# First attention: two transposed thirds of the weights ahead of the next scores, the projections behind the last third, the subtraction in two halves

## The reference, cut to what matters

```python
x = _layernorm(x + _L0_attn_ref(x, L0_attn_W_Q, L0_attn_W_K, L0_attn_W_V, L0_attn_W_O, L0_attn_b_Q, L0_attn_b_K, L0_attn_b_V, L0_attn_virtual_k, L0_attn_virtual_v), axis=-1)
x = _layernorm(x + _L0_xattn_ref(x, ctx_768, ...), axis=-1)
...
```

## Time and profile before

| | before |
|---|---|
| median of three runs | 4582.13 us |
| the profiled execution | 4580.66 us |
| its span in the profile | 4578.9 us |
| first scores (L275) to last | 152.5 to 867.5 us |
| TensorE busy, share of the span | 84% |
| mean granted TensorE clock | 0.92 |

### The profile page before, as it was taken

The page is one execution under the profiler, slowest core; times in us unless marked ns, Lnnn a source line. Parts: engine busy times, 40 slices in busy tenths (PEclk is TensorE's granted clock), DMA queues, the critical chain, the costliest instruction groups (busy, mean ns, idle before and its releaser), DMA issues. The chain is left out here.

```text
span 4578.9 us, 84527 instructions
## 1 busy us (share of the span) xinstructions
PE 3831.4 (84%) x33378; PEld 2565.5 (56%) x33378; DVE 2800.7 (61%) x7503; ACT 2112.3 (46%) x3569; POOL 1172.6 (26%) x819
## 2 busy tenths in 40 slices
PE   0688888888899879998999996654779999598999
PEld 0466666566556556664555554433547776465665
DVE  9577777666899756666565554985242222476555
ACT  4466666544333225555555544441364444354332
POOL 3444444222344311002455452321110000010000
PEclk9999999999999859999999998776689999798999
DMA  2222222100000001000000000003300000000000
GB/s 93 45 49 48 47 47 48 22 1 1 1 1 1 1 12 41 2 1 1 2 2 2 2 2 1 15 21 114 121 1 1 1 1 1 28 2 2 1 10 10
DMA packets 59436, 91.90 MB, mean 20 GB/s; under 512 B 16306, under 2 KB 42628, under 8 KB 57796
## 3 DMA queue, kind: packets, MB, share of 16 engines
q1 hardware_dynamic: 54916, 80.88, 7.5%
q10 hardware_dynamic: 4128, 5.64, 0.4%
HBM read 42.30 MB, written 10.62 MB: 12 GB/s over the span
## 5 line engine op out<-in xcount | busy, mean ns | idle before, releaser
L853 PE MATMUL banks<-XT,weight_region 128*128 128x512 f32 x1696 | 781.2, 599 | 2.3 <-DVE T L1229 2.3
L875 PEld LDWEIGHTS banks<-weight_region,HT 128*128 128x128 f32 x4672 | 560.5, 192 | 151.5 <-issue 91.7
L1252 DVE SCALAR_TENSOR_TENSOR x_res<-banks,WT,x_res 128x128 f32<-128x128 f32 x1056 | 297.1, 343 | 489.4 <-PE banks L875 449.6
L875 PE MATMUL banks<-weight_region,HT 128*128 128x128 f32 x4672 | 570.1, 276 | 21.6 <-DVE HT L1240 15.2
L853 PEld LDWEIGHTS banks<-XT,weight_region 128*128 128x128 f32 x1696 | 305.8, 193 | 288.5 <-issue 283.2
L1005 ACT ACTIVATE HT<-banks,weight_region 128x512 f32<-128x512 f32 x256 | 173.1, 687 | 240.0 <-PE banks L853 233.7
L1068 POOL TENSOR_TENSOR FNM<-FNM,FRS 128x8 f32<-128x8 f32 x16 | 4.6, 286 | 1014.4 <-ACT FRS L964 1014.4
L458 DVE TENSOR_REDUCE MX<-banks 128x8 f32<-128x1152 f32 x128 | 173.1, 1352 | 115.8 <-PE banks L275 113.8
L384 ACT COPY PT<-banks 128x384 f32<-128x384 f32 x384 | 171.4, 480 | 131.5 <-PE banks L285 129.7
L1643 ACT COPY PT<-banks 77x512 f32<-77x512 f32 x256 | 142.8, 582 | 186.9 <-PE banks L1565 186.8
L1096 POOL TENSOR_TENSOR T<-T,T 128x512 f32<-128x512 f32 x128 | 162.6, 1272 | 210.6 <-ACT T L1028 208.1
(11 more groups left out here) (472 smaller groups left out, 8589.7 us busy)
## 6 DMA issues: line engine op xcount, KB each, us to landing
FL<-RAW SPq DMA_DIRECT2D x512, 64.0 KB, 2.3
T<-s4d_k_dram SPq DMA_DIRECT2D x8, 1024.0 KB, 5.8
weight_region<-in_l_ffn__w_dram SPq DMA_DIRECT2D x2, 2048.0 KB, 8.6
film_dram<-F SPq DMA_DIRECT2D x8, 512.0 KB, 2.9
weight_region<-in_l_ffn__w_dram ACTq DMA_DIRECT2D x2, 2048.0 KB
FO<-film_dram SPq DMA_DIRECT2D x8, 512.0 KB, 4.1
x_res<-in_x_dram SPq DMA_DIRECT2D x1, 2048.0 KB
weight_region<-in_l_ffn__w_dram SPq DMA_DIRECT2D x2, 1024.0 KB, 10.6
```

The lines of the kernel that those rows point to most:

```text
L853: nc.tensor.matmul(PS[:, q % 4, :], w, xt, start=True, stop=True).then_inc(s.h_ps, 1)
L875: ins = nc.tensor.matmul(PS[:, 4 + u % 2, b * P:(b + 1) * P], HT[:, u % 2, j, b * P:(b + 1) * P], w2[j], start=j == 0, stop=j == len(w2) - 1)
L1252: ins = nc.vector.scalar_tensor_tensor(R[:, t, :], PS[:, 4 + u % 2, b * P:(b + 1) * P], WT[:, t, e:e + 1], R[:, t, :], ALU.mult, ALU.add)
```

## The change

TensorE, step n: T0 and T1 of step n-2 come first, then the scores of step n, then T2, then the due items, then both mixes. The ring's order is T0, T1, T2, items. ScalarE copies T0, T1 and T2 ahead of the items. VectorE subtracts in two halves, banks 0 and 1 (new semaphore `sub_a`), then banks 2 and 3 (`sub`); TensorE's project and first two mask matmuls wait for `sub_a`, the last two for `sub`.

```diff
-                order += [("T0", n - 2), ("T1", n - 2)]
+                order += [("T0", n - 2), ("T1", n - 2), ("T2", n - 2)]
             order += due(n)
-            if n >= 2:
-                order.append(("T2", n - 2))
...
                     if n >= 1:
-                        pe.wait_ge(s.sub, n)
+                        pe.wait_ge(s.sub_a, n)
                     if n >= 2 * NR and n % NR == 0:
                         project(n // NR - 2)
                     for i in range(4):
+                        if i == 2 and n >= 1:
+                            pe.wait_ge(s.sub, n)
                         nc.tensor.matmul(PS[:, i, 0:2 * K], IDB[:], MASK[:].rearrange("p a k -> p (a k)"), start=True, stop=False)
...
                 for n in range(N + NR + 1):
+                    live = 2 <= n < N + 2
+                    if live:
+                        weights_T(n - 2, 0)
+                        weights_T(n - 2, 1)
                     if n < N:
                         scores(n)
                     elif n % NR == 0:
                         pe.wait_ge(s.sub, N)
                         project(n // NR - 2)
-                    live = 2 <= n < N + 2
                     if live:
-                        weights_T(n - 2, 0)
-                        weights_T(n - 2, 1)
+                        weights_T(n - 2, 2)
                     for item, p in due(n):
                         produce(item, p)
                     if live:
-                        weights_T(n - 2, 2)
                         mix(n - 2, 0)
-                    if live:
                         mix(n - 2, 1)
...
                     if live:
                         weights(3 * (n - 2))
                         weights(3 * (n - 2) + 1)
+                        weights(3 * (n - 2) + 2)
                     for item, p in due(n):
                         take(item, p)
-                    if live:
-                        weights(3 * (n - 2) + 2)
...
-                    nc.vector.tensor_tensor(SM[:, n % 3, 1:9, :].rearrange("p (a i) k -> p i a k", a=2), sc[:, :, :, 0:P],
-                                            bc(MX[:, n % 2].unsqueeze(3), [P, 4, 2, P]), ALU.subtract).then_inc(s.sub, 1)
+                    main = SM[:, n % 3, 1:9, :].rearrange("p (a i) k -> p i a k", a=2)
+                    for h, done in ((0, s.sub_a), (2, s.sub)):
+                        nc.vector.tensor_tensor(main[:, h:h + 2], sc[:, h:h + 2, :, 0:P], bc(MX[:, n % 2, h:h + 2].unsqueeze(3), [P, 2, 2, P]),
+                                                ALU.subtract).then_inc(done, 1)
```

More of the change, by code:

```diff
@@ L185, in due @@
         return [(item, n // NPR + 1) for item in TAKE[n % NPR]] if n // NPR + 1 < NP else []
-    with sublayer(nc, "cst vkc one xt_ps xt kq_ps raw flip0 flip1 cosm sinm rot v_ps v s_ps mx sub ex pt_ps pt z_ps shuf lnz rz zt o_ps res" + LN) as (s, ctx):
+    with sublayer(nc, "cst vkc one xt_ps xt kq_ps raw flip0 flip1 cosm sinm rot v_ps v s_ps mx sub_a sub ex pt_ps pt z_ps shuf lnz rz zt o_ps res" + LN) as (s, ctx):
         sb = E.scratch(ctx)
```

## The result

The changed kernel takes 4543.17 us (median of four runs, 4541.02 to 4546.31) against 4584.33 of the kernel before (four runs, one more than on record ahead of the prediction, 4579.23 to 4591.21): a ratio of 0.991, 95% interval 0.9893 to 0.9927, 41 us less. Forecast were 28 us less, 4554, with a range of 4533 to 4575. The profiled execution took 4541.47 us, its span is 4539.7.

What follows compares the result with a forecast made beforehand. TensorE's program was taken as the bound: 38.0 us of work and 6.9 of waits in a 44.90 us window. Windows of 42.9, 2.0 less, over 14 windows give 28 us less: 4554, range 4533 to 4575.

Steps and rivals of the forecast that it cites:

- The two waits that were to go: TensorE, each step: 0.45 us between T1 and T2 ahead of the projection, 0.41 ahead of the second mix; both go.
- The new one: TensorE ahead of T2's transposes, waiting for ScalarE's copy of T0: some 2.8 us a window, 40 in all.
- u(n): The moment at which step n's last queries-by-keys matmul is issued on TensorE; the prediction lays out its times from it.
- The wait for V's slot: TensorE at T1, whose ring slot V still holds until VectorE takes it out: 0.86 us, once each window.
- The rotary product: VectorE at n % 8 = 6: its wait for DMAs, 2.11 us before, stays over 2 us.
- Project in step 7: TensorE waits about 1.0 us for the subtraction's first half, pushed late by the rotary product's DMAs.
- TensorE's work, 38.0 us a window: TensorE's work without waits: eight steps of 3.38, nine items of 0.97, X 0.3, two projects of 0.97.
- gaps between scores: TensorE, from u(n) to u(n+1): 3.38 plus items, project and T2's wait; eight gaps sum to 42.62 us.
- The halves: VectorE's subtraction split in two: second starts 0.60 us behind the first, counted at nothing beyond 0.08 in T2's wait.
- No change: Rival: within 0.3%, T2's wait on TensorE eats the gain, 4571 us; chance 0.14.
- slower: Rival: VectorE's second half stretches by 0.74 us while TensorE writes masks, 4596 us; chance 0.06.
- most waits go: Rival: T2 does not wait for ScalarE's copy, about 40 us a window, 4513 us; chance 0.06.

Runs made afterwards that it cites:

- the last third: Kernel before with only T2 moved ahead of the due items (ring, TensorE and ScalarE alike), one subtraction: 4555.67 us, 0.994.
- the later rotary product: Changed kernel with the third rotary product of a window in VectorE's step 7 in place of step 6: 4552.31 us, 0.9937.
- the kernel with all three: Changed kernel with T0 and T1 copied ahead of the exponential, V ahead of the shuffle, third rotary product in step 7: 4516.75 us, 0.9859.

## Why the prediction was right, and where its size was off

**The direction and the mechanism held.** The two waits that were to go went. The new one was forecast at some 2.8 us a window, 40 in the 14 windows, ahead of T2's transposes; it is 37.0 in them. The ends of these waits were laid out well: from u(n) to T2 of step n+1 it is 5.38 for n = 5 (forecast 5.58), 7.17 for n = 7 (7.16), 4.69 for n = 0 (4.74) and 4.70 for n = 4 (4.74). Only n = 1 is far off, 5.98 (5.58). The wait for V's slot was forecast at 0.86: T0 is issued at 432.17 and T1 at 433.38, 1.21 apart where T0 holds 0.36, which makes 0.85 (forecast 0.86); the bracket says 0.67.

```profile
432.17 0.55 PE L285 MATMUL banks<-sb_c_ident,SM 128*128 128x128 f32 x3
433.38 0.55 PE L285 MATMUL banks<-sb_c_ident,SM 128*128 128x128 f32 x3 [0.67 <-DVE VZ L439]
433.77 1.06 PE L308 MATMUL banks<-weight_region,ZT 128*128 128x128 f32 x8
434.66 0.65 PE L271 MATMUL banks<-maskb,identb 128*128 128x288 bf16 x4
```

The rotary product waits for its DMAs over 2 us still (2.33). Project in step 7 stands longer than the 1.0 that was forecast: TensorE is through with T1 at 410.20 + 0.71 = 410.91 and starts it at 412.38, 1.47. The end of that wait hangs on the landing and came when it was laid out to come, 13.93 us behind u(5); TensorE came to it 0.5 sooner.

**The term that was mis-sized is TensorE's work, 38.0 us a window.** Windows 2 to 15 take 41.7 us on average by the starts of the scores, not 42.9; before it was 44.9. The sum of work had taken the two mixes at 0.77 (0.41 + 0.36, "where nothing is waited for"), from a row whose 16 matmuls had a hidden wait; they hold 0.58 (405.49 to 406.07). With the rounding up to 3.38 that is 0.2 x 8 = 1.6 a window too much. The transposes were 0.05 too cheap, twice a step (T0 and T1 0.71 in place of 0.66, T2 0.38 in place of 0.33), 0.8 the other way. A K or Q item whose weights load ahead of it holds 0.86 (408.45 to 409.31), not 0.97, and so does V (430.42 to 431.28); a project then holds 0.89 (433.77 to 434.66). As far as they stand so in this window, and with 0.01 off each mask row, that is some 0.6. Together 36.6 in place of 38.0. With waits of 5.1 in place of 4.9 this gives the 41.7, and 14 windows x 1.2 are the 16 us by which this stretch beat the forecast. The rest of the kernel gave some 5 back, which is no more than one execution differs from the next; no run shows whether it is more than that.

By the same reading the waits of the earlier trace rows were larger than the prediction read them: the two mixes and what stands between them take 1.18 (417.24 to 418.42), 0.60 more than 0.58, and not 0.41 more. So more was to be won from the last third than the prediction saw. That this is why it gives 28 us is argued from the rows.

Per step, gaps between scores in one window of the changed kernel (from 402.48 on), the forecast in brackets: step 6, 4.88 (5.11); step 7, 6.57 (6.31); step 0, 4.19 (4.53); step 1, 5.61 (5.61); step 2, 4.61 (4.35); step 3, 6.90 (7.54); step 4, 4.20 (4.35); step 5, 4.74 (4.82). T2 waits in steps 5, 6, 0 and 1, as forecast, and in step 2 in place of step 3. A wait that is shorter in one step comes up in the next; the sum moves little.

**The halves.** Counted at nothing, they are worth nothing (4543.17 and 4543.04 with and without). They start 0.60 apart and the pair takes 1.28 where the single one took 1.21, about as laid out from the earlier trace rows (1.29). The Trainium skill's rule (VectorE: DVE Perf Modes, The DRAIN you can't avoid), by which a next operation waits for an empty pipe, gave 4564. The same section says that an operation that is not held starts earlier, which the prediction passed over; the pair's start, 0.08 ahead of the end of the first half, agrees with that.

**The rivals.** No change and slower fell with the result. Slower needed the second half to stretch while TensorE writes masks. In 40 of 128 steps masks do start while the second half runs, and it takes 0.67 to 0.68 us in them, as everywhere; the 256 halves have a mean of 680 ns.

```profile
L467 DVE TENSOR_TENSOR SM<-banks,MX 128x512 f32<-128x512 f32 x256 | 163.5, 680 | 0.0
```

That most waits go (4513) did not happen by the change, but its condition, T2 not waiting for the copy, could be made: with the copies ahead of the exponential the time is 4517.

What stays open: why the later rotary product gains nothing even in the windows without a layer norm as long as T2 waits behind ScalarE (41.6 to 42.7 us, against 41.1 to 41.8 in the changed kernel). In such a window from 330 us on, step 7 takes 5.99 in it and 6.00 in the changed kernel, and steps 1 and 2 are longer (6.40 and 5.50 against 5.60 and 4.61). What holds them is not shown.

## What to carry to other kernels

A run of matmuls in one row can span a semaphore wait shorter than their overlap; before a row is taken as the price of unhindered work, look at the weight loads' row and at the producer's end. And count the waits: as many as there are steps means that no step is free of it. When an order is changed on the engine that sets the pace, look at the engines that empty its buffers as well: here 26 of 65 us lay in ScalarE's program, where two copies stood behind an exponential. And before a long operation is moved on a helper engine, look at what it sets going beside the operations next to it, and at the clock behind the wait that comes of it: the later rotary product cost some 9 us in a step with the scaling and gained some 10 with the scaling elsewhere.

## What the runs showed of the hardware

The scaling of the layer norm (L124, SBUF to SBUF, 128 elements) has a median of 0.34 us over the kernel. In the first attention its mean is longer, in the kernel with all three (first row) more than in the changed kernel (second):

```profile
L124 DVE TENSOR_SCALAR x_res<-x_res,ln_mv,ln_rstd 128x128 f32<-128x128 f32 x32 | 29.4, 980 | 0.6 <-ACT ln_rstd L116 0.6
...
L124 DVE TENSOR_SCALAR x_res<-x_res,ln_mv,ln_rstd 128x128 f32<-128x128 f32 x32 | 19.7, 674 | 0.6 <-ACT ln_rstd L116 0.6
```

980 against 674 ns, with the same work. What differs is how many of them run beside a GpSimd operation: 28 of 32 against 14. Those beside one have a mean of 1.07 and 1.11 us, the others 0.34 in both kernels, and one that stands beside a whole GpSimd operation takes 1.3 and ends 0.08 behind it. GpSimd's own keep their 1.26 to 1.28. VectorE's operations on PSUM beside the same GpSimd operations keep their length too (1.34 at 283.44 above). The Trainium skill (SBUF — State Buffer, Who interferes with whom) says that VectorE in a two-port mode, which such an operation can enter, and GpSimd exclude each other for a whole instruction. The trace agrees, with three of VectorE's four each ending 0.08 behind one of GpSimd's.

TensorE is held some 0.1 us more by a product whose first weight load could not start ahead of it, 0.97 against 0.86 for the same four records. At 408.45 the load starts 0.11 ahead of the product; at 404.21, behind T2's wait, and at 429.45, where no bracket shows a wait, it starts with it. A sum of work has to take such a term from rows of the same kind.

The granted clock of TensorE stays at 1.00 through waits of 1.3 us (412.38 in the changed kernel), and is 0.51 and 0.50 behind waits of 3.46 and 2.81.
